# Linear attention plus a top-2 LoRA layer: transposes of k and of x moved from TensorE to the DMA engines

## The reference, cut to what matters

```
xn  = layernorm(x)
q   = elu(xn Wq^T)+1 ;  k = elu(xn Wk^T)+1 ;  v = xn Wv^T          (8 heads of 64)
S_t = g S_{t-1} + k_t v_t^T ;  z_t = g z_{t-1} + k_t                 (per head, over 2048 tokens)
y_t = (S_t^T q_t) / (z_t . q_t + 1e-6) * sigmoid(xn Wg^T + b)
attn = y Wo^T
ffn  = xn Wlin^T + b_lin + sum over the top 2 of 8 experts of  w_e (xn left_e) right_e
out  = x + attn + ffn
```

## Time and profile before

| what | us |
|---|---|
| median of 3 runs | 265.98 (265.62 to 266.72) |
| the profiled execution | 264.92 |
| its span on the slowest core (core 3) | 263.9 |
| TensorE busy | 243.6 (92%) |
| VectorE busy | 162.8 (62%) |
| ScalarE busy | 79.5 (30%) |
| GpSimd busy | 61.7 (23%) |

### The profile page before, as it was taken

How to read it: one execution, slowest core, us unless ns; L and a number is a source line. 1 busy time by engine, 2 the same in 40 slices (tenths; PEclk the granted TensorE clock), 3 DMA queues, 4 the chain that set the end, 5 groups by cost and what they waited for, 6 DMA issues and landing times.

```text
span 263.9 us, 5412 instructions; the slowest of 8 cores (262.6 to 263.9 us)
## 1 busy us (share of the span) xinstructions
PE 243.6 (92%) x1768; PEld 122.6 (46%) x1768; DVE 162.8 (62%) x425; ACT 79.5 (30%) x132; POOL 61.7 (23%) x99
## 2 busy tenths in 40 slices
PE   0369999999889999999999999999999999999995
PEld 0233444454444555454545454445545555544442
DVE  5646374858766667565664657546556685686622
ACT  2644857375445222324333022111111201000000
POOL 2773000030505501314050403021304030333000
DMA  6999999999994022120404022122222123343223
GB/s 183 238 142 253 243 166 226 208 194 178 254 345 149 0 83 79 70 92 0 161 1 157 4 82 79 79 83 81 79 82 82 80 80 106 137 137 105 82 97 142
DMA packets 9615, 33.25 MB, mean 126 GB/s; under 512 B 1458, under 2 KB 1778, under 8 KB 9332
## 3 DMA queue, kind: packets, MB, share of 16 engines
q1 hardware_dynamic: 6692, 22.27, 24.8%
q0 software_dynamic: 2896, 10.64, 21.4%
HBM read 32.00 MB, written 8.39 MB: 153 GB/s over the span
## 4 chain that ended last, share of the span: by engine, by line
PE 84%; DVE 7%; issue 3%; DMA 3%; ACT 1%; SPq 0%; DVEq 0%; ACTq 0%
PE PJ L340 26%; PE L L362 17%; PE L L406 8%; PE PJ L333 7%; PE PJ L362 4%; PE L L340 4%; DMA x_sb<-x 3%; PE T L311 3%; PE L L333 2%; PE SY L354 2%; PE PJ L406 2%; PE T L347 2%; PE SY L378 1%; PE T L319 1%; PE T L392 1%
## 5 line engine op out<-in xcount | busy, mean ns | idle before, releaser
L362 PE MATMUL L<-wlin_sb,xnfm 128*128 128x512 bf16 x208 | 49.2, 379 | 0.0
L298 POOL TENSOR_SCALAR S_blk<-S_sb,small_s 128x260 bf16<-128x260 f32 x30 | 28.8, 973 | 85.8 <-DVE S_sb L775 85.6
L362 PEld LDWEIGHTS L<-wlin_sb,xnfm 128*128 128x128 bf16 x208 | 19.8, 98 | 23.2 <-issue 0.8
L844 ACT ACTIVATE e_sb<-PJ 128x512 bf16<-128x512 f32 x28 | 16.5, 593 | 42.1 <-PE PJ L340 40.6
L608 DVE TENSOR_SCALAR e_sb<-e_sb 128x512 bf16<-128x512 bf16 x32 | 9.4, 294 | 28.7 <-ACT e_sb L844 28.7
L820 ACT ACTIVATE xn_tm<-x_sb,nmr,rstd 128x1024 bf16<-128x1024 f32 x16 | 19.9, 1241 | 23.6 <-POOL nmr L254 22.1
L406 PE MATMUL L<-wo_sb,ygfm 128*128 128x512 bf16 x104 | 26.7, 379 | 0.0
L340 PE MATMUL PJ<-xnfm,wg_sb 128*128 128x512 bf16 x112 | 26.6, 379 | 0.0
L340 PE MATMUL PJ<-xnfm,wq_sb 128*128 128x512 bf16 x112 | 26.6, 380 | 0.0
L340 PE MATMUL PJ<-xnfm,wk_sb 128*128 128x512 bf16 x112 | 26.6, 380 | 0.0
L333 PE MATMUL PJ<-wv_sb,xnfm 128*128 128x512 bf16 x96 | 24.6, 400 | 0.0
(11 more groups left out here) (115 smaller groups left out, 357.0 us busy)
## 6 DMA issues: line engine op xcount, KB each, us to landing
ro_sb<-x SPq DMA_DIRECT2D x16, 512.0 KB, 4.0
out<-ro_sb SPq DMA_DIRECT2D x15, 512.0 KB, 2.7
x_sb<-x SPq DMA_DIRECT2D x10, 512.0 KB, 8.8
x_sb<-x POOLq DMA_DIRECT2D x6, 512.0 KB, 21.3
wlin_sb<-wlin POOLq DMA_DIRECT2D x1, 2048.0 KB, 38.9
wv_sb<-wv POOLq DMA_DIRECT2D x4, 256.0 KB, 10.9
wq_sb<-wq POOLq DMA_DIRECT2D x2, 512.0 KB, 18.2
wk_sb<-wk POOLq DMA_DIRECT2D x2, 512.0 KB, 24.7
```

Source lines behind the costliest of these rows:

```text
L298: GP.tensor_scalar(S_blk[:, :].rearrange("p (q w) -> p q w", q=4)[:, :, 65 * e : 65 * e + 65], S_sb[:, :].rearrange("p (q w) -> p q w", q= ...
L362: TE.matmul(lb(c, n)[:, :], xnk(k, c), wlin_sb[:, D * k + 512 * n : D * k + 512 * n + 512], start=False, stop=False)
L844: SE.activation(e_sb[:, 512 * (n % 2) : 512 * (n % 2) + 512], bank[:, :], AF.Exp).then_inc(ac_e, 1)
```

## The change

Chunks 8 to 15 of x and k of blocks 1 to 3 are transposed by DMAs that SP issues, from SBUF to SBUF; chunks 0 to 7 and k of block 0 stay on TensorE. `xtr` (from chunk 8) and `ktr` (from chunk 4; renamed `kpe`) leave TensorE, and `xev_s` leaves ACT. A DMA `xt(c)` moves 256 KB and replaces eight transposes and one copy; a DMA `kt(b, m)` moves 128 KB: one of four head pairs of a whole block, issued when `phi` has finished it. DVE reads k from the new buffer `ktr_sb` when all four of a block have landed. Who waited for the copy (`ac_xev`) now waits for the DMA (`d_xt`). The wait for `dv_gate` stands ahead of `state` instead of `ktr` from chunk 4 on. The rings of residual rows and of gated y shrink to 3 and 4. SP's queue gets a new order: `xt(8)` and `xt(9)` stand behind the two copies into `right_sb` and ahead of the wait for `wlin`, and then one pass after another has its loads, its `xt`, its `kt` and its store.

```
-YR = 6
+YR = 4
+RR = 3
...
+        def xt(c):
+            SY.wait_ge(ac_xn, c + 1)
+            SY.dma_start_transpose(xdst(c), xn_tm[:, (c % 2) * D : (c % 2) * D + D]
+                                   ).then_inc(d_xt[c], 16)
+
+        def kt(b, m):
+            SY.wait_ge(dv_k, 4 * b + m + 1)
+            if b >= 2:
+                SY.wait_ge(dv_ktm, 4 * b - 4)
+            SY.dma_start_transpose(
+                ktr(b).rearrange("p (s f) -> p s f", s=4)[:, :, 128 * m : 128 * m + 128],
+                fm(kfm, b)[:, 512 * m : 512 * m + 512]).then_inc(d_kt[b], 16)
+
+        def store(c):
+            SY.wait_ge(dv_out, 2 * c + 2)
+            SY.dma_start(out_d[128 * c : 128 * c + 128, :], ro(c)).then_inc(d_o[c], 16)
...
         SY.dma_start(right_sb[97:98, :], lo_s[96:97, :]).then_inc(d_lo, 16)
-        SY.wait_ge(d_wl, 16)
-        load_x(12)
-        load_x(13)
-        load_res(0)
-        load_res(1)
-        SY.wait_ge(d_wo, 16)
-        load_x(14)
-        load_x(15)
-        load_res(2)
-        load_res(3)
-        for c in range(NCH - 1):
-            SY.wait_ge(dv_out, 2 * c + 2)
-            SY.dma_start(out_d[128 * c : 128 * c + 128, :], ro(c)).then_inc(d_o[c], 16)
-            if c + 4 < NCH:
-                SY.wait_ge(d_o[c], 16)
-                load_res(c + 4)
+        xt(8)
+        xt(9)
+        for c in range(NCH):
+            b, s = c // 4, c % 4
+            lo = c - LAG
+            if c == 0:
+                SY.wait_ge(d_wl, 16)
+            if c + 12 < NCH:
+                load_x(c + 12)
+            if c < RR:
+                load_res(c)
+            else:
+                SY.wait_ge(d_o[c - RR], 16)
+                load_res(c)
+            if c + 10 < NCH:
+                xt(c + 10)
+            if c < NCH - 4:
+                kt(b + 1, s)
+            if lo >= 0:
+                store(lo)
+        store(NCH - 2)
...
     def vslot(c):
-        TE.wait_ge(ac_xev, c + 1)
+        TE.wait_ge(d_xt[c + 8], 16)
         TE.wait_ge(dv_q, c + 5)
         vproj(c + 8, PJ[0])
...
             TE.wait_ge(dv_k, 4 * b + 4)
-            if c == 0:
-                TE.wait_ge(dv_xev, 8)
-            else:
-                TE.wait_ge(dv_gate, c)
-            ktr(c)
+            if c < 4:
+                if c == 0:
+                    TE.wait_ge(dv_xev, 8)
+                else:
+                    TE.wait_ge(dv_gate, c)
+                kpe(c)
...
-                if s == 0 and b > 0:
-                    TE.wait_ge(ac_xev, 4 * b)
+                if s == 0:
+                    for ci in range(4 if b > 0 else 0):
+                        TE.wait_ge(d_xt[4 * b + 4 + ci], 16)
...
-            if c + 8 < NCH:
-                if c > 0:
-                    TE.wait_ge(ac_xev, c)
-                ...
-                xtr(c + 8)
...
                 TE.wait_ge(dv_ktm, c + 1)
+                if c >= 4:
+                    TE.wait_ge(dv_gate, c)
                 state(c)
...
-            VE.wait_ge(pe_ktr, c + 1)
+            if c < 4:
+                VE.wait_ge(pe_ktr, c + 1)
+                ktile = T1[:, 0:512]
+            else:
+                VE.wait_ge(d_kt[b], 64)
+                ktile = ktr(b)[:, 512 * s : 512 * s + 512]
...
         SE.wait_ge(d_x[c], 16)
-        if c >= 2:
+        if c >= 10:
+            SE.wait_ge(d_xt[c - 2], 16)
+        elif c >= 2:
             SE.wait_ge(pe_xtr, c - 1)
...
-            if c + 8 < NCH:
-                xev_s(c + 8)
```

More of the change, by code:

```diff
@@ L65, in build_core @@
     th_g = A("th_g", [128, 2 * 2048], F32)
-    ro_sb = A("ro_sb", [128, 4 * D], F32)
+    ro_sb = A("ro_sb", [128, RR * D], F32)
     xn_tm = A("xn_tm", [128, 2 * D], BF16)
@@ L72, in build_core @@
     qt_sb = A("qt_sb", [128, 2 * 512], BF16)
+    ktr_sb = A("ktr_sb", [128, 2 * 2048], BF16)
     ktm_sb = A("ktm_sb", [128, 512], BF16)
@@ L128, in build_core @@
     d_o = [sem(f"d_o{c}") for c in range(NCH)]
+    d_xt = [sem(f"d_xt{c}") for c in range(NCH)]
+    d_kt = [sem(f"d_kt{b}") for b in range(NB)]
     d_r = [sem(f"d_r{c}") for c in range(NCH)]
@@ L171, in ro, with ktr @@
     def ro(c):
-        return ro_sb[:, (c % 4) * D : (c % 4) * D + D]
+        return ro_sb[:, (c % RR) * D : (c % RR) * D + D]
+    def ktr(b):
+        return ktr_sb[:, (b % 2) * 2048 : (b % 2) * 2048 + 2048]
     def yg(c):
@@ L307, in xtr @@
     def xtr(c):
-        t = TT[c % 2] if c < 8 else T0
+        t = TT[c % 2]
         TE.wait_ge(ac_xn, c + 1)
@@ L324, in tht @@
     def tht(b):
-        TE.wait_ge(dv_th, b + 1)
         for ci in range(4):
@@ L343, in fproj, with kpe @@
             ins.then_inc(s, 1)
-    def ktr(c):
+    def kpe(c):
         for p in range(4):
@@ L521, in pe_program @@
             if more:
-                if s == 0 and b > 0:
-                    TE.wait_ge(ac_xev, 4 * b)
+                if s == 0:
+                    for ci in range(4 if b > 0 else 0):
+                        TE.wait_ge(d_xt[4 * b + 4 + ci], 16)
+                    if b == 0:
+                        TE.wait_ge(dv_xev, 8)
                 if c == 0:
@@ L567, in pe_program @@
             if s == 2 and more:
-                if c + 8 < NCH:
-                    TE.wait_ge(ac_xev, c + 1)
-                else:
-                    TE.wait_ge(ac_thr, b + 1)
+                TE.wait_ge(ac_thr, b + 1)
                 tgp(b + 1)
             if s == 0:
-                if c + 8 < NCH:
-                    TE.wait_ge(ac_xev, c + 1)
+                TE.wait_ge(dv_th, b + 1)
                 tht(b)
@@ L734, in dve_program @@
             more = c < NCH - 4
-            VE.wait_ge(pe_ktr, c + 1)
+            if c < 4:
[4 more added lines that the diff above has]
+                ktile = ktr(b)[:, 512 * s : 512 * s + 512]
             if c > 0:
                 VE.wait_ge(pe_st, c)
-            VE.tensor_tensor(ktm_sb[:, :], T1[:, 0:512], dpk[:, :],
-                             ALU.mult).then_inc(dv_ktm, 1)
+            VE.tensor_tensor(ktm_sb[:, :], ktile, dpk[:, :], ALU.mult).then_inc(dv_ktm, 1)
             VE.wait_ge(pe_sc, c + 1)
@@ L821, in xn @@
                       bias=nmr[:, c : c + 1], scale=rstd[:, c : c + 1]).then_inc(ac_xn, 1)
[L823 to L826, removed]
     def vev(c, bank):
```

## The result

The changed kernel takes 272.1 us (median) against 265.9: a ratio of 1.023, interval 1.020 to 1.026. The profiled execution took 272.3 us, its slowest core spans 271.3 us. 270.5 was forecast.

The account below looks back on a forecast made before the run. From about pass 2 the kernel was taken as one stream of TensorE work, 92% busy. 264.9 - 6.2 (stream) + 8.3 (stall) + 2.5 (clock) = 269.5 us profiled, 270.5 for the median; range 260.0 to 277.0.

Parts of the forecast that it names:

- The gain of the stream: Work leaving TensorE from pass 0 on: x transposes 3.1, k transposes 2.4, passes 13 to 15 0.2, stalls 0.5; together 6.2 us.
- the 0.5 that was forecast: Pass 1: a late exp on ScalarE (0.31 us) and a wait of `ktr(1)` (0.25) both go; 0.5 us gained.
- the 0.2 that was forecast: Passes 13 to 15, where VectorE decides: 0.2 us gained for the three together (0 to 0.9).
- The term put at nothing: Steady part: waits for `xt` and `kt` DMAs cost nothing, as 2.7 and 4.0 us for 512 KB fit the cover.
- The cover of the fourth `kt`: Last k transpose of a block, before `av`: its DMA may take 4.4 us before anybody waits.
- The stall at chunk 8: Pass 0: `vslot(0)` waits for `xt(8)`, landing at 73.5 (72.2 to 76.5); 8.3 us lost (7.0 to 11.3).
- land one behind the other: SP's queue before pass 0: DMAs land in turn whatever their size; none issued after 60 landed before 72.
- takes the place of that next load: SP's queue: `xt(8)` replaces the load issued at 63.43, which took 10.1 us, so it lands at 73.5.
- three rivals: For `xt(8)`: landing with the backlog (the forecast, 0.60), not held by the queue (0.24), or slow in itself (0.14).
- The clock: TensorE behind the stall in pass 0: idling lowers its speed; 2.5 us lost (bounds 0 to 4).
- B: The queue doesn't hold the transposes, `xt(8)` lands by 64.4, nothing is lost: 260.3 us, about 2% faster; chance 0.24.
- C: A transpose is slow in itself, 10.1 us anywhere: `xt(8)` lands at 82.3, median 279, or 296 with `kt`; chance 0.14.

## Why the prediction was right, and where not

- **The gain of the stream**, 6.2 us forecast, 5.1 measured. Passes 2 to 11 gave 4.6 for 5.1 (six `xtr` and nine `ktr`); pass 1 gave 0.5, its `xtr`; the waits behind the stall gave the 0.5 that was forecast (`ytr(0)` to the head of pass 1 takes 2.17 us with the clock kept up, for 2.72 before); from `av` of pass 12 to `av` of pass 15 it is 22.64 us for 22.89, the 0.2 that was forecast. The term put at nothing was wrong: from the scores to `av` pass 12 takes 3.10 us for 2.34, 0.8 lost. The cover of the fourth `kt` was worked out for block 1 (4.4 us). In block 3 phi of k ended at 223.82 and `av` could have started at 229.4, where its eight `lin` matmuls ended; less the same 2.0 us leaves 3.6, and the DMA took 3.9, with 0.3 more between phi, issue, landing and the multiplication. "I take nothing" held for the blocks before and not for this one.
- **The stall at chunk 8**, the step that decided: right in place, cause of the wait and nearly in size. Landing 73.5 forecast, 74.8 measured; lost 8.3 forecast, 10.7 measured without the clock. Of the 2.4 between them 1.5 is the later start of the projection (75.06 for 73.6) and 0.9 that this execution came to the wait earlier.
- **Why it lands there**: here the working failed. It said that DMAs of SP "land one behind the other" and that `xt(8)` "takes the place of that next load". Moved to the head of the queue it still took 15.1 us, and a plain copy at the head took 12.0; without `wo` beside them the same DMA took 5.9 to 6.7 on the slowest cores. None of the three rivals had that cause either. The row of the small copy, 12.5 us, was read as a queue's length; it landed at 72.5, and `wo` at 72.1 (issued 24.90, 47.2 us to landing). The trace before held a row against the queue, the other small copy:

```profile
59.39 0.61 SPq L206 DMA_DIRECT2D right_sb<-lo_s  x1
```

```profile
DMA to landing us min/median/max: 10.2/10.2/10.2
```

It landed at 69.6, ahead of the load in front of it, which the prediction has at 72.2: not one behind the other. Both readings give 72 to 75 in the kernel as changed, so that the number came out is in part luck; as a guide to a repair the first would have misled. Which of the sixteen engines, or which turn between q0 and q1, makes the last piece late, no run here settles.
- **The clock**, 2.5 us forecast: 2.3 by the time of the run that keeps TensorE at work, and 2.75 by the rows of the two traces (1.64 in the projection, 1.11 in the transposes and matmuls behind it). The half of the rule of "TensorE: Matmul & The Clock Gate", section "What's actually happening", in the Trainium skill that the rows before could not show, that idling brings the throttle back, the trace agrees with: 0.50 granted after the idle stretch.
- **The rivals.** B fell by the landing. C fell by the medians of 4.4 and 2.5 us to landing. By the Trainium skill's "VectorE: DVE Perf Modes", section "The three transpose paths", the eight blocks of an `xt`, one after another, would take an estimated 10.5 us; the trace has 4.4 for all eight and disagrees. The Trainium skill's "Advanced Engine Details and Errata", section "X-Bar Transpose (TRN2)", has transposes as fast as regular DMAs: a store of 512 KB took 2.7 us in the same run and a transpose of half the size 4.4 (3.1 at best), so that rule is nearer, and still too good.

## What to carry to other kernels

Work moved from a full engine to the DMA engines is gained in the steady part and must be looked at where the DMA engines are still full: the first use decides, and here two chunks left on the old path turned 2.3% slower into 1.6% faster. When a small transfer is slow, a run that puts it first and a run that takes the neighbour away tell order from sharing; in the trace alone, set its landing beside the landing of what runs next to it, not only beside what was issued ahead of it. A late result is best read behind the work that doesn't need it: the masks first, then the multiplication that waits for a DMA.

## What the runs showed of the hardware

- What SP issued from SBUF to SBUF between 54.9 and 63.5 us landed with the last weight that POOL had queued: 256 KB, copied or transposed, within 0.3 us for the plain copy and 0.8 to 3.1 us behind it for `xt(8)`, on all cores of the five runs.
- Issuing a DMA transpose held SP's queue for 1.2 us each in the quiet part, and 10.1 us for `xt(8)` behind two loads and two copies while the weights ran; at the head of the queue, in the same stretch, 1.55 us. Nothing else was issued meanwhile.
- The changed kernel's DMA had 16434 packets under 512 bytes, the kernel before 1458: a transpose is cut into small packets (3.7 MB over the 15000 more, some 245 bytes each).
- Behind waits of 11.52, 3.92 and 2.55 us on TensorE the granted clock was 0.50, and the matmuls there ran at half pace.
